# A graph layer and a routed FFN on one core: adjacency handed over transposed, plain fp32 product, work moved between engines

## The reference

```python
neighbor_sum = jnp.einsum('bnm,bmd->bnd', adjacency, x)     # x is layer-normed
agg = epsilon * x + neighbor_sum
h = jnp.einsum('bnd,dh->bnh', agg, W1) + b1                  # 128 -> 512
h = jax.nn.silu(_rmsnorm(h, rms_weight))
out = jnp.einsum('bnh,hd->bnd', h, W2) + b2                  # 512 -> 128
...
gate_scores = jnp.einsum('bsd,ed->bse', x, Wg) + bg          # x is layer-normed again
topk_scores, topk_idx = jax.lax.top_k(gate_scores, K)        # K = 2 of E = 8
...
for e in range(E):
    h = jax.nn.relu(jnp.einsum('bsd,hd->bsh', x, W1[e]) + b1[e])
    y = jnp.einsum('bsh,dh->bsd', h, W2[e]) + b2[e]
    out = out + combine[..., e:e + 1] * y
```

## Time and profile before

| what | value |
|---|---|
| median of 3 runs | 638.59 us (638.51 to 656.82) |
| span of the profiled execution | 637.5 us |
| PE (TensorE, products) busy | 583.9 us, 92% |
| PEld (TensorE, weight loads) busy | 536.8 us, 84% |
| DVE (VectorE) busy | 422.9 us, 66% |
| ACT (ScalarE) busy | 368.7 us, 58% |
| POOL (GpSimd) busy | 445.1 us, 70% |
| DMA | 127.29 MB, mean 200 GB/s |
| mean granted TensorE clock | 0.989 |

### The profile page before, as it was taken

The page is one execution under the profiler, slowest core; times in us unless marked ns, Lnnn a source line. Parts: engine busy times, 40 slices in busy tenths (PEclk is TensorE's granted clock), DMA queues, the critical chain, the costliest instruction groups (busy, mean ns, idle before and its releaser), DMA issues.

```text
span 637.5 us, 14755 instructions
## 1 busy us (share of the span) xinstructions
PE 583.9 (92%) x4379; PEld 536.8 (84%) x4379; DVE 422.9 (66%) x1255; ACT 368.7 (58%) x932; POOL 445.1 (70%) x728
## 2 busy tenths in 40 slices
PE   1899999898998998989999799999999999999873
PEld 0688898787897887878988698999999999999851
DVE  2658989788897887978877764445444444444454
ACT  4377586775866857757568444555545545545411
POOL 4334388978879789797977787676676676677650
PEclk9999999999999999999999899999999999999997
DMA  7970244223441344314551677667677666667698
GB/s 268 394 275 19 116 167 158 91 101 151 167 153 46 135 166 162 120 57 161 164 164 35 238 239 273 252 240 259 240 253 261 250 244 252 249 238 266 212 410 344
DMA packets 42614, 127.29 MB, mean 200 GB/s; under 512 B 8155, under 2 KB 20872, under 8 KB 40488
## 3 DMA queue, kind: packets, MB, share of 16 engines
q1 hardware_dynamic: 33320, 108.88, 47.0%
q0 software_dynamic: 8640, 16.93, 8.0%
q10 hardware_dynamic: 576, 0.53, 0.3%
HBM read 61.19 MB, written 24.02 MB: 134 GB/s over the span
## 4 chain that ended last, share of the span: by engine, by line
PE 56%; POOL 16%; DVE 8%; issue 6%; ACT 6%; DMA 5%; SPq 1%; POOLq 0%; DVEq 0%; ACTq 0%
PE ps_y L760 9%; PE ps_g L760 9%; POOL slots L1050 7%; PE ps_y L589 5%; PE ps_agg L526 4%; PE ps_agg L527 4%; PE ps_t L532 3%; POOL x_all L1043 3%; PE ps_agg L750 2%; PE ps_h L750 2%; PE ps_h L527 2%; PE ps_h L526 2%; PE ps_t L735 2%; DVE rows L1201 2%; PE ps_agg L629 2%
## 5 line engine op out<-in xcount | busy, mean ns | idle before, releaser
L1121 POOL DMA_INDIRECT parts<-adj_in x142 | 139.5, 982 | 71.3 <-ACT adj_in L955 55.2
L1050 POOL DMA_INDIRECT slots<-rows,dest x128 | 132.5, 1035 | 22.8 <-issue 22.6
L955 ACT ACTIVATE adj_in<-adj_in,share 128x128 f32<-128x128 f32 x142 | 49.4, 395 | 116.8 <-issue 104.4
L813 ACT ACTIVATE adjT_hi<-ps_t 128x512 fp32r<-128x512 f32 x128 | 75.8, 593 | 46.5 <-PE ps_t L532 45.2
L1163 DVE TENSOR_TENSOR adjT_lo<-ps_t,adjT_hi 128x512 fp32r<-128x512 f32 x128 | 87.4, 687 | 22.1 <-ACT adjT_hi L813 18.6
L532 PEld LDWEIGHTS ps_t<-ident,adj_in 128*128 128x128 f32 x512 | 77.6, 191 | 24.1 <-issue 13.3
L532 PE MATMUL ps_t<-ident,adj_in 128*128 128x128 f32 x512 | 78.7, 277 | 13.8 <-POOL adj_in L1022 13.8
L1419 DVE TENSOR_TENSOR adjT_lo<-ps_t,adjT_hi 128x256 fp32r<-128x256 f32 x71 | 30.1, 424 | 74.1 <-ACT adjT_hi L937 74.1
L526 PE MATMUL ps_agg<-adjT_hi,xn_split 128*128 128x512 f32 (+1 forms) x162 | 70.2, 433 | 1.0 <-ACT adjT_hi L813 1.0
L760 PE MATMUL ps_y<-W2e,hb 128*128 x576 | 70.4, 275 | 0.6 <-issue 0.6
L760 PEld LDWEIGHTS ps_y<-W2e,hb 128*128 128x128 f32 x576 | 67.6, 192 | 0.8 <-issue 0.8
(11 more groups left out here) (241 smaller groups left out, 1413.0 us busy)
## 6 DMA issues: line engine op xcount, KB each, us to landing
adj_in<-in_adj SPq DMA_DIRECT2D x16, 2048.0 KB
wcur<-expert_w SPq DMA_DIRECT2D x54, 578.0 KB
xn_split<-expert_w SPq DMA_DIRECT2D x17, 578.0 KB
adj_in<-slots SPq DMA_DIRECT2D x71, 130.0 KB
expert_w<-parts SPq DMA_DIRECT2D x8, 512.0 KB, 9.8
out<-x_all SPq DMA_DIRECT2D x8, 512.0 KB, 6.5
x_all<-in_x SPq DMA_DIRECT2D x1, 3072.0 KB, 20.1
parts<-adj_in POOLq DMA_INDIRECT x142
```

The source lines that it names most:

```text
L813: act.activation(adjT_hi[m % 2][:, :], ps_t[m % 2][:, :], ACT.Copy).then_inc(s_hi, 1)
L955: ins = act.activation(ye[ku][:, j, :], yb[ku % 2][:, j, :], ACT.Copy, scale=share[ku][:, j:j + 1])
L1050: pool.indirect_dma_start(out=slots, out_offset=bass.IndirectOffsetOnAxis(ap=dest[q % 2][:, c, j:j + 1], axis=0), in_=rows[q % 2][:, c, j, ...
L1121: pool.indirect_dma_start(out=parts, out_offset=bass.IndirectOffsetOnAxis(ap=goes[u % 8][:, j, :], axis=0), in_=ye[ku][:, j, :], in_offset ...
```

## The change

The host hands over the adjacency with its last axes swapped and cut as the kernel uses it, the weights transposed and laid out as used, and all small constants in one block. In the kernel:

- `M(m)` is one plain fp32 product of 512 columns. Its transposes, ScalarE's 128 copies, VectorE's 128 subtractions and the splits of the normed x are gone.
- Epsilon is added to the diagonal blocks by VectorE, between `second_choice` and `places`.
- `transpose_hidden` and `first_layer` use four banks (`h_bank`); `rank` stands before `M(7)`, behind it before.
- GpSimd does `ln2_factors`, then four of the eight scatters, then `rms_factors`, then the other four.
- The experts' weights come in on SyncE's queue in steps 2 and 3, and their high and low parts are made in steps 4 to 11, one expert in each, at the end of the step's work of ScalarE and VectorE.
- VectorE takes the layer-norm statistics of group g-2 before it adds b1; they came behind the first two additions before.
- The fourth `wcur` has a buffer of its own.

```diff
+        adj_in = [sb(f"adj_in{i}", [P, TPB, GTOK]) for i in range(2)]
+        xn_both = sb("xn_both", [P, 2, TPB, D])
+        xn = [xn_both[:, i, :, :] for i in range(2)]
...
+        wcur += [sb("wcur3", [P, WROW], FP32R)[:, :]]
...
-        F1raw = adj_in[0][:, :, :].rearrange("p a n -> p (a n)").rearrange("p (c d) -> p c d", d=D)
-        F2raw = adj_in[1][:, :, :].rearrange("p a n -> p (a n)").rearrange("p (e h) -> p e h", h=H)
...
+        h_bank = (ps_h[0], ps_h[1], ps_t[0], ps_t[1])
...
+            def load_group(g):
+                wait(sp, s_mm, g - 1)
+                sp.dma_start(adj_in[g % 2][:, :, :], adjT[g]).then_inc(s_adj[g % 2], 16)
...
-            sp.wait_ge(s_tp, TPB * (NG - 1))
-            sp.dma_start(F1raw, F1.rearrange("e (c p) d -> p (e c) d", p=P)).then_inc(s_F1, 16)
-            sp.wait_ge(s_tp, TPB * NG)
-            sp.dma_start(F2raw, F2.rearrange("e d h -> d e h")).then_inc(s_F2, 16)
+            for g in range(2, NG):
+                load_group(g)
+                if g == 2:
+                    sp.dma_start(W1e[:, :, 1, :].bitcast(FP32), F1T[:, :, :]).then_inc(s_F1, 16)
+                elif g == 3:
+                    sp.dma_start(W2e[:, :, :], F2T[:, :, :]).then_inc(s_F2, 16)
+                    sp.dma_start(biases[:, :, :], biases_in[:, :, :]).then_inc(s_fb, 16)
...
             def step(g, par, b):
                 def M(m):
-                    if has(g, 0):
-                        if par == 0 and m % (TPB // 2) == 0:
-                            pe.wait_ge(s_xl, b * 2 + m // (TPB // 2) + 1)
-                        pe.wait_ge(s_hi, TPB * g + m + 1)
-                        two_passes(ps_agg[par][:, :], xn_hi[:, m, :], xn_lo[:, m, :], adjT_hi[m % 2][:, :],
-                                   start=(m == 0))
-                        pe.wait_ge(s_lo, TPB * g + m + 1)
-                        pe.matmul(ps_agg[par][:, :], xn_hi[:, m, :], adjT_lo[m % 2][:, :],
-                                  start=False, stop=(m == TPB - 1)).then_inc(s_mm, 1)
-                        if m + 2 < TPB:
-                            transpose_rows(par, m + 2)
-                        elif has(g, -1):
-                            if m + 2 == TPB:
-                                pe.wait_ge(s_epsadd, 4 * g + 8)
-                            transpose_rows(1 - par, m + 2 - TPB)
+                    if m == 0:
+                        pe.wait_ge(s_xn, 2 * b + 2)
+                        pe.wait_ge(s_epsadd, g + 1)
+                        wait(pe, s_agg, g - 1)
+                    ins = pe.matmul(ps_agg[par][:, :], xn[b % 2][:, m, :], adj_in[par][:, m, :],
+                                    start=(m == 0), stop=(m == TPB - 1))
+                    if m == TPB - 1:
+                        ins.then_inc(s_mm, 1)
+                M(0)
                 if has(g, 1):
                     pe.wait_ge(s_aggh, g)
-                    if isinstance(g, int) and g == 1:
+                    if g == 1:
                         pe.wait_ge(s_W1l, 1)
-                    first_layer(g - 1, (0, 1), ps_h)
-                M(0)
+                    first_layer(g - 1, (0, 1))
+                M(1)
                 if has(g, 1):
-                    first_layer(g - 1, (2, 3), ps_h)
-                M(1)
+                    first_layer(g - 1, (2, 3))
                 M(2)
                 M(3)
                 if has(g, 2):
-                    q = g - 2
-                    transpose_normed(q, ps_y)
+                    transpose_normed(g - 2, ps_y)
                 M(4)
                 if has(g, 2):
-                    q = g - 2
-                    gate(q)
+                    gate(g - 2)
                 M(5)
                 if has(g, 1):
                     pe.wait_ge(s_hn, g)
                     pe.wait_ge(s_hna, g)
                     transpose_hidden(g - 1, (0, 1, 2, 3))
                 M(6)
+                if has(g, 2):
+                    rank(g - 2)
                 M(7)
-                if has(g, 2):
-                    q = g - 2
-                    rank(q)
                 if has(g, 1):
-                    q = g - 1
-                    second_layer(q, range(HC))
-                if isinstance(g, int) and g == 0:
-                    pe.wait_ge(s_const, 16 * 9)
-                    pe.transpose(ps_g[:, 0:NS], small[:, :], ident[0:NS, 0:NS]).then_inc(s_smallT, 1)
+                    if g == 1:
+                        pe.wait_ge(s_const, 16)
+                    second_layer(g - 1, range(HC))
...
+            first_layer(q, range(GT))
+            transpose_normed(q - 1, ps_y)
+            gate(q - 1)
+            keep_busy(ps_agg[0], 20)
             pe.wait_ge(s_hn, NG)
             pe.wait_ge(s_hna, NG)
...
+            transpose_hidden(q, (0, 1, 2, 3))
             rank(q - 1)
...
+            second_layer(q, range(HC))
+            keep_busy(ps_agg[0], 30)
             transpose_normed(q, ps_y)
...
             gate(q)
...
+            keep_busy(ps_agg[0], 12)
...
+            def high_weights(e):
+                if e == 0:
+                    act.wait_ge(s_F1, 16)
+                act.activation(W1e[:, e, 0, :], W1e[:, e, 1, :].bitcast(FP32), ACT.Copy).then_inc(s_wTa, 1)
...
             def step(g, par, b):
...
+                if has(g, 1):
+                    for j in range(GT):
                         sum_squares(g - 1, j)
...
                 if has(g, 2):
...
+                    normed(g - 2, ps_y)
                 if has(g, 1):
                     scale_hidden(g - 1)
...
                 if par == 1 and has(g, -1):
                     normalise(b + 1, 0)
...
+                if has(g, 1):
+                    for c in range(HC):
+                        hidden(g - 1, c)
                 if par == 1 and has(g, -1):
                     normalise(b + 1, 1)
...
+                act.wait_ge(s_mm, g + 1)
+                wait(act, s_h, 4 * g)
+                act.activation(aggT_hi[:, :], ps_agg[par][:, :], ACT.Copy).then_inc(s_aggh, 1)
                 if has(g, 2):
...
+                    second_rows(g - 2)
+                if 4 <= g < 4 + E:
+                    high_weights(g - 4)
...
-            def add_eps(g, par, b):
-                pool.wait_ge(s_adj[par], 16 * b + 16)
-                for j in range(GT):
-                    own = adj_in[par][:, j, par * GT + j::TPB]
-                    pool.tensor_tensor(own, own,
-                                       eps_ident[:, :], ALU.add).then_inc(s_epsadd, 1)
...
             def step(g, par, b):
                 order.step((g + 1) * 6)
-                if has(g, 3):
-                    pool.wait_ge(s_dest, g - 2)
-                    pool.wait_ge(s_row2, g - 2)
                 if has(g, 2):
                     ln2_factors(g - 2)
-                if has(g, 1):
-                    rms_factors(g - 1)
-                if has(g, -1):
-                    add_eps(g + 1, 1 - par, b + par)
-                if isinstance(g, int) and g == 0:
-                    pool.wait_ge(s_const, 16 * 9)
-                if par == 0 and has(g, 0):
+                if par == 0:
                     pool.wait_ge(s_xn, b * 2 + 2)
                     pool.sem_inc(s_turn, 1)
                     if not has(g, 3):
                         x_plus_b2(b)
                 if has(g, 3):
-                    for c in range(2):
-                        scatter_rows(g - 3, c, b if par == 0 else None)
+                    pool.wait_ge(s_dest, g - 2)
+                    pool.wait_ge(s_row2, g - 2)
+                    scatter_rows(g - 3, 0, b if par == 0 else None)
+                if has(g, 1):
+                    rms_factors(g - 1)
+                if has(g, 3):
+                    scatter_rows(g - 3, 1, b if par == 0 else None)
...
+            def add_eps(g):
+                par = g % 2
+                dve.wait_ge(s_adj[par], 16 * (g // 2) + 16)
+                if g == 0:
+                    dve.wait_ge(s_epsid, 1)
+                for j in range(GT):
+                    own = adj_in[par][:, par * GT + j, j * P:(j + 1) * P]
+                    ins = dve.tensor_tensor(own, own, eps_ident[:, :], ALU.add)
+                ins.then_inc(s_epsadd, 1)
...
             def step(g, par, b):
                 order.step((g + 1) * 22)
...
                 if has(g, 2):
...
+                    ln2_stats(g - 2)
                     ln2_aggregate(g - 2)
                 if has(g, 1):
...
+                    add_b1(g - 1, (0, 1))
                 if par == 0 and has(g, -2):
...
+                    dve.wait_ge(s_mv1, b + 1)
+                    dve.sem_inc(s_turn_dve, 1)
+                    if b <= 1:
                         dve.wait_ge(s_xs if b == 0 else s_xr, 16)
                     ln1_stats(b + 1, 0)
                 if has(g, 1):
...
+                    add_b1(g - 1, (2, 3))
                 if has(g, 2):
...
+                    normed_rows(g - 2)
+                if g == 0:
+                    dve.wait_ge(s_W1h, 1)
```

(17 more changed lines are left out.)

367 lines of the change are left out of this document (85 added, 282 removed).

## The result

The changed kernel took 653.26 us (median of 5 runs, 647.74 to 655.80), the kernel before 640.04 us (median of 5). The ratio is 1.022 (95% interval 1.014 to 1.029). The prediction was 640 us, with a range of 625 to 656. (Single executions of a kernel can fall some per cent above the rest; the ratios leave these out.)

The account below looks back on a forecast made before the run. Bound: TensorE's work in even steps, GpSimd's queue in odd; afterwards a chain through GpSimd's scatters. Span 637.5 - 10.2 - 1.0 = 626.3 us, 627.4 as median, plus 12.6 for clock falls: 640 us, range 625 to 656.

Parts of the forecast that it names:

- the forecast's own case: Whole kernel: GpSimd's chain sets the steps and the clock drops in 3 to 10 gaps; 633 to 647 us, chance 0.48.
- falls: TensorE's granted clock drops to its lower level behind a wait: 7 of 13 gaps at 1.8 us each, 12.6 us.
- rival B: First part's steps: the clock falls in nearly every gap, 11 to 13 falls, 647 to 665 us; chance 0.20.
- That loop without falls: Steps 3 to 15: chain between engines with RMS factors behind four scatters, 20.6 (even) and 19.4 us (odd), 264.2 with splits.
- The splits: Weights' high and low parts, steps 4 to 11: VectorE's subtraction delays steps 5 to 12 by 0.6 us each, 4.8 us.
- the bare steps: Steps of the first part without the weights' splits: 20.6 us (even) and 19.4 us (odd).
- The wait ahead of the hidden transposes: TensorE idle until hidden rows are scaled: 3.4 us (even), 2.2 (odd), 0.6 more in eight steps; 2.2 to 4.0 us.
- the 0.3 us ahead of the ranks: TensorE in each step: ranks, moved ahead of `M(7)`, wait for both choices, which adds 0.3 us.
- Rivals C and D: C: RMS factors don't wait the scatters' full time, near 587 us, chance 0.06; D: adjacency product 1.0 us, 0.3 a step.
- Between the parts: After step 15, before the second part's tiles: 2 us lost to 3 us gained, taken as 1 us gained.
- The start: First three steps, no scatters in the way: first product at 15 us, end of step 2 at 58.2 against 70.2.
- second part: TensorE's dense row of work on 71 tiles, with the same passes and weight loads: taken as unchanged.

Follow-up runs that it names:

- The kernel with the filler: Changed kernel plus 20 unread identity transposes on TensorE before its wait for the scaled hidden rows: 673.67 us (first chip), 668.83 us (third; 0.940 of the kernel before).
- the second chip: Changed kernel run again unaltered, on a chip where the kernel before took 640.10 us: 652.93 us, ratio 1.022 to the kernel before.
- the last kernel: Changed kernel with RMS factors before all scatters, 12 filler transposes, and only GpSimd's two small groups exchanged between the parts: 650.41 us (third chip), no ratio.
- its sister on the second chip: Changed kernel with RMS factors first, 12 filler transposes, small groups exchanged and four scatters moved ahead between the parts: 610.23 us, 0.955 of the kernel before.

## Why the prediction was right, and where it was off

The measured 653.26 us lies in the range of 625 to 656, but the forecast's own case, 3 to 10 falls and 633 to 647 us, is not what happened. The range holds it because it takes in the lower half of rival B.

**The mechanism held.** The step was forecast as a loop: `second_layer`, addition and statistics, layer-norm factors, four scatters, RMS factors, scaling, transposes, `second_layer`. That loop without falls was put at 20.6 and 19.4 us, 264.2 us for 13 steps. The kernel with the filler, which has the same loop and a clock of 1.00, took 266.0. The splits were forecast at 4.8 us, and the steps that have them are 3.4 longer; the bare steps at 20.6 and 19.4, and they are 21.2 and 19.4. The wait ahead of the hidden transposes was forecast at 2.2 to 4.0 us and is 2.2 to 3.1. By its own sum those figures are all the idle time of a step (20.6 - 17.2 and 19.4 - 17.2), the 0.3 us ahead of the ranks among it, and so a little high for this one wait. Leaving out three eighths of the product changed nothing, and taking the RMS factors out from behind the scatters took away the wait. Rivals C and D are out (`M(m)` takes 0.86 us).

**The term that was mis-sized is the number of falls.** "I take it that 7 of the 13 gaps make it fall ... at 1.8 us each: 12.6 us." There were 11 in the profiled execution and 13 on the second chip, at 1.58 and 1.59 us: 17.4 and 20.65 us. The price was nearly right and the count was not. My reason for so few odd steps was the gap of 2.35 us that cost nothing before; in the changed kernel gaps of 2.24 to 2.67 us did. The length of the gap alone does not decide: in the first trace steps 6 and 7 waited 3.01 and 2.53 us without a fall, and step 13 fell behind 2.24 us. The kernel before had five gaps of 2.28 to 2.35 us, in its odd steps 5 to 13, and kept its clock behind all of them. The windows view over its steps 3 to 15:

```profile
66.40:328.80 262.40, 249.86 (x1727) 222.36 (x1725) 224.65 (x730) 180.75 (x385) 212.10 (x325) 1.00 0.37 126
```

The error was to carry what a gap of that length does over to a gap in another place of another kernel. What makes one gap cost and another of the same length not is not shown. Strictly, rival B is what happened, in its lower half (647 to 665, 651 the likeliest, given 0.20). The section of the Trainium skill that the prediction names (TensorE: Matmul & The Clock Gate, "HAM oscillation — how this bites in real kernels") describes a loop whose every round waits and starts the next one at the lower clock. These runs agree in that: with a wait in every round, 11 and 13 of 13 rounds went on at the lower clock. The waits of its example are mostly longer than these (2.24 to 3.05 us), and its remedy is another order of the loop or a larger product; the filler is a remedy that only these runs show.

**Between the parts** I took 1 us gained, within 2 lost and 3 gained; 2.7 us were lost (with the ends as the prediction read them, 50.6 us were forecast for the stretch and it took 54.5). Only GpSimd's scatters were followed there. TensorE's and the small factor groups' order were not: `ln2_factors(14)` stands behind `rms_factors(15)`, which waits for the squares of group 15, and that is the wait of 6.49 us. The same order stands in the kernel before, but there TensorE had weights to transpose in that time (from 336.05 us on).

**The start** was 2.7 us better than forecast: `second_layer` of step 1 began at 34.60 us. The first product began at 12.98 us where 15, between 13.5 and 18, was taken; the rest of the stretch took 42.5 us where 43.2 was forecast.

**The sum** of the misses against the forecast's span of 638.9 (626.3 + 12.6): start -2.7, loop +1.8, falls +4.8, between the parts +3.9, second part -0.7, together +7.1, which is 646.0. The other runs were 5 to 8 us longer at a lower mean clock. The second trace has 3.3 us more in steps 3 to 15 than the first, so part of that may be more falls; only the one execution is traced.

**Open.** Which gaps make the clock fall, and which don't. And why the kernel before takes 66 to 69 us longer on two of the chips. In the eight traces taken there, the stretch from the end of step 15 to tile 7's rows takes 63 to 70 us, against 52 to 59 in the six others, and the rest behind it 259 to 289 us, against 253 to 254. The stretch from tile 0 to the end is 306.3 us for the last kernel, against 276.4 for its sister on the second chip, and on the first chip the page shows some 215 GB/s in the second part where the first trace of the changed kernel has some 250. The kernel before itself was not traced there.

## What to carry to other kernels

When several engines hand work round in a loop, follow one round by hand before pricing an engine's savings: a product made cheaper by a quarter was worth nothing in the steady steps here, and the place of one 1.3 us instruction group in a queue was worth 31 to 36 us. Put what others wait for ahead of what nobody waits for, and look at every copy of the order, the one behind the loop too. Where a wait of TensorE must stay, work that nobody reads in that wait was worth 1.6 us a time; it belongs only where there is a wait.
